# Minimum and maximum of the key gap moved from GpSimd to VectorE, with a new instruction order, in a fused recurrent block (RWKV attention gated by a feed-forward branch)

## The reference

```
xn = layernorm(x)                                  # over channels
shifted = xn moved one token later (zero first)
k, v, r = (xn*mix + shifted*(1-mix)) @ Wk, Wv, Wr  # three mixes
r = sigmoid(r)
# per channel, a scan over the 512 tokens, kept stable by a running maximum mx
td = -exp(time_decay)
out   = (e1*num + e2*v) / (e1*den + e2)            # e1 = exp(mx-max_out), e2 = exp(k+tf-max_out)
mx'   = max(mx + td, k)
num'  = exp(mx+td-mx')*num + exp(k-mx')*v
den'  = exp(mx+td-mx')*den + exp(k-mx')
s = (r * out) @ Wo
h = relu(xn @ w1[0] + b1[0]);  y = h @ w2[0] + b2[0]   # 128 -> 512 -> 128
g = silu(layernorm(xn + y) * gamma + beta)
result = x + s * g
```

## Time and profile before

| what | value |
|---|---|
| median of 3 runs | 134.46 us (133.47 to 134.66) |
| the profiled execution, its own time | 134.19 us |
| its span, first to last instruction | 132.4 us |
| busy: PE, DVE, ACT, POOL | 108.0, 104.2, 99.8, 93.3 us |
| mean granted TensorE clock | 0.955 |

### The profile page before, as it was taken

The page is one execution under the profiler, slowest core; times in us unless marked ns, Lnnn a source line. Parts: engine busy times, 40 slices in busy tenths (PEclk is TensorE's granted clock), DMA queues, the critical chain, the costliest instruction groups (busy, mean ns, idle before and its releaser), DMA issues. The chain is left out here.

```text
span 132.4 us, 1678 instructions
## 1 busy us (share of the span) xinstructions
PE 108.0 (82%) x340; PEld 57.8 (44%) x340; DVE 104.2 (79%) x208; ACT 99.8 (75%) x154; POOL 93.3 (70%) x124
## 2 busy tenths in 40 slices
...
DVE  1796988998449999387899997099956999887972
...
POOL 2069799999996799789969999999929428204000
...
GB/s 121 264 344 144 2 0 0 0 2 5 0 0 2 0 0 0 0 0 14 68 0 0 5 0 79 0 0 0 0 2 82 0 51 29 0 2 84 0 158 79
DMA packets 9450, 5.09 MB, mean 38 GB/s; under 512 B 480, under 2 KB 9184, under 8 KB 9440
## 3 DMA queue, kind: packets, MB, share of 16 engines
...
q10 hardware_dynamic: 560, 0.40, 1.1%
...
...
## 5 line engine op out<-in xcount | busy, mean ns | idle before, releaser
L620 PE MATMUL ps_z<-hid,w_c 128*128 128x512 f32 x64 | 30.8, 599 | 0.2 <-issue 0.2
L585 PE MATMUL ps_up<-xT_hi,w_hi 128*128 128x512 f32 x32 | 20.8, 651 | 7.2 <-POOL xT_hi L340 2.6
L445 ACT ACTIVATE hid<-ps_up,vec 128x512 f32<-128x512 f32 x32 | 21.1, 680 | 4.7 <-PE ps_up L587 4.6
L368 POOL TENSOR_SCALAR gap_max<-gap,td 128x512 f32<-128x512 f32 x8 | 16.6, 2072 | 1.7 <-DVE gap L745 1.2
L620 PEld LDWEIGHTS ps_z<-hid,w_c 128*128 128x128 f32 x64 | 11.4, 189 | 12.5 <-issue 9.5
L327 POOL TENSOR_SCALAR xn<-x_sb,neg_mean,rstd 128x128 f32<-128x128 f32 x28 | 15.0, 546 | 0.2 <-POOL rstd L313 0.2
L587 PE MATMUL ps_up<-xT_lo,w_hi 128*128 128x512 f32 x32 | 13.1, 409 | 0.0
L586 PE MATMUL ps_up<-xT_hi,w_lo 128*128 128x512 f32 x32 | 13.0, 406 | 0.0
L585 PEld LDWEIGHTS ps_up<-xT_hi,w_hi 128*128 128x128 f32 x32 | 6.5, 202 | 14.9 <-issue 9.5
L752 DVE TENSOR_TENSOR_SCAN den<-e_keep,e_new 128x512 f32<-128x512 f32 x8 | 10.5, 1312 | 2.4 <-ACT e_new L473 2.3
L376 POOL TENSOR_TENSOR dv<-v_sb 128x512 f32<-128x512 f32 x8 | 9.3, 1157 | 4.4 <-ACT v_sb L487 4.4
...
## 6 DMA issues: line engine op xcount, KB each, us to landing
...
```

The lines of the kernel that those rows point to most:

```text
L368: pool.tensor_scalar(gap_max[n][:, :], gap[n][:, :], td[:, :], HIGHEST, ALU.max, ALU.min).then_inc(done["gap_max"], 1)
L445: act.activation(hid[b % 2][:, f, :], ps_up[f % 2][:, :], ACT.Relu, bias=vec[:, B1_COLUMN + f:B1_COLUMN + f + 1]).then_inc(done[f"hid{f}"], 1)
L585: pe.matmul(dst, hi, xT_hi[n][:, :], start=True, stop=False)
L620: ins = pe.matmul(ps_z[b % 2][:, :], w2_c[:, f, :], hid[b % 2][:, f, :], start=False, stop=last, skip_group_check=True)
```

## The change

`gap_min` and `gap_max` leave POOL's list and go to DVE's, as one `tensor_scalar` each with one comparison instead of two. Their waits are the same. POOL's list has 70 steps in place of 86, DVE's 160 in place of 144; PE's and ACT's have as many steps as before (124 and 154, with the same 16 table loads). The order of the steps is new on all four engines. On POOL three waits are added that the new order needs. The diff, with the lists of PE and ACT cut:

```diff
 ACT = mybir.ActivationFunctionType
 LN_EPS = 1e-5
 MX_START = -1e38
-LOWEST, HIGHEST = -3.4028234e38, 3.4028234e38
 WARM_UP = 11
...
     "pe": """
-        T:0 b2m up0:0 up3:0 k:0 up2:0 up1:0 z3:0 z2:0 z0:0 T:1 z1:0 v:0 up1:1 var:0 up0:1 k:1 up3:1 r:0
...
+        b2m T:0 up0:0 up1:0 k:0 up2:0 up3:0 z1:0 z0:0 z3:0 T:1 z2:0 v:0 var:0 up2:1 up1:1 k:1 up0:1 r:0 T:2
...
     "act": """
-        ln_exp ve0 rs0 w1_hi neg_td xT:0 xT_hi:0 hid0:0 wo hid3:0 hid2:0 hid1:0 xT:1 e_keep:0 e_new:0 sq:0
...
+        ln_exp ve0 rs0 w1_hi neg_td xT:0 xT_hi:0 hid0:0 hid1:0 hid3:0 hid2:0 e_new:0 e_keep:0 wo xT:1 sq:0
...
     "dve": """
-        bnA:0 bnB:0 aggr1:0 norm1:0 bn:1 aggr1:1 one_minus cols xT_lo:0 w2_sum ink:0 bn:2 inr:0 aggr1:2
-        inv:0 mx:0 gap:0 bn:3 bn:4 aggr1:3 bn:5 xT_lo:1 den:0 ink:1 rel:0 inr:1 mx:1 zn:0 inv:1 aggr1:4
-        gap:1 dev:0 xT_lo:2 adev:0 ink:2 wkv:0 gated:0 inr:2 den:1 zn:1 rel:1 inv:2 mx:2 ink:3 gap:2 xT_lo:3
-        bn:6 inr:3 dev:1 aggr1:5 mx:3 gap:3 adev:1 wkv:1 inv:3 den:2 zn:2 bn:7 rel:2 aggr1:6 prod:0 den:3
-        xT_lo:4 res:0 ink:4 gated:1 dev:2 inv:4 adev:2 wkv:2 zn:3 inr:4 mx:4 rel:3 prod:1 gated:2 ink:5
-        aggr1:7 gap:4 dev:3 xT_lo:5 adev:3 wkv:3 inr:5 mx:5 gap:5 zn:4 res:1 inv:5 den:4 gated:3 ink:6 rel:4
-        xT_lo:6 prod:2 mx:6 dev:4 adev:4 gap:6 wkv:4 inv:6 den:5 inr:6 zn:5 den:6 res:2 rel:5 rel:6 xT_lo:7
-        ink:7 prod:3 dev:5 gated:4 mx:7 res:3 adev:5 gap:7 wkv:5 gated:5 inv:7 inr:7 prod:4 den:7 dev:6
-        adev:6 wkv:6 rel:7 res:4 zn:6 gated:6 prod:5 dev:7 prod:6 adev:7 wkv:7 res:5 gated:7 res:6 zn.a:7
-        zn.b:7 prod.a:7 prod.b:7 res.a:7 res.b:7
+        bnA:0 bnB:0 aggr1:0 one_minus norm1:0 bn:1 cols aggr1:1 w2_sum xT_lo:0 inv:0 ink:0 bn:2 inr:0 mx:0
+        bn:3 gap:0 aggr1:2 gap_min:0 gap_max:0 bn:4 aggr1:3 den:0 bn:5 xT_lo:1 inr:1 ink:1 rel:0 zn:0 inv:1
+        mx:1 aggr1:4 gap:1 dev:0 gap_max:1 ink:2 xT_lo:2 adev:0 gap_min:1 wkv:0 mx:2 gated:0 gap:2 den:1
+        gap_min:2 zn:1 gap_max:2 inr:2 inv:2 bn:6 prod:0 rel:1 den:2 xT_lo:3 ink:3 dev:1 aggr1:5 aggr1:6
+        adev:1 mx:3 wkv:1 rel:2 inr:3 zn:2 inv:3 gated:1 bn:7 gap:3 res:0 gap_min:3 gap_max:3 dev:2 xT_lo:4
+        adev:2 ink:4 wkv:2 inv:4 den:3 inr:4 zn:3 prod:1 rel:3 gated:2 mx:4 res:1 aggr1:7 gap:4 ink:5
+        xT_lo:5 gap_min:4 dev:3 gap_max:4 mx:5 prod:2 adev:3 gap:5 wkv:3 gap_min:5 gated:3 inr:5 zn:4 inv:5
+        gap_max:5 den:4 res:2 ink:6 rel:4 den:5 xT_lo:6 mx:6 dev:4 gap:6 adev:4 gap_min:6 wkv:4 inr:6 inv:6
+        gap_max:6 zn:5 prod:3 den:6 gated:4 res:3 rel:5 ink:7 rel:6 xT_lo:7 dev:5 prod:4 adev:5 mx:7 wkv:5
+        gap:7 res:4 gated:5 inr:7 gap_min:7 inv:7 prod:5 gap_max:7 dev:6 den:7 adev:6 wkv:6 rel:7 res:5
+        gated:6 zn:6 prod:6 dev:7 res:6 adev:7 wkv:7 zn.a:7 gated:7 zn.b:7 prod.a:7 prod.b:7 res.a:7 res.b:7
     """,
     "pool": """
-        w1_lo neg_mean1:1 Bk:0 Br:0 Bv:0 w2_c rstd1:1 norm1:1 gap_min:0 gap_max:0 xT_hi:1 neg_mean1:2 Bk:1
-        Br:1 rstd1:2 Bv:1 norm1:2 dv:0 keep:0 xT_hi:2 Br:2 Bk:2 gap_max:1 neg_mean1:3 gap_min:1 rstd1:3 Bv:2
-        norm1:3 dv:1 neg_mean1:4 Bk:3 Br:3 xT_hi:3 keep:1 rstd1:4 gap_max:2 gap_min:2 neg_mean1:5 Bv:3
-        gap_max:3 gap_min:3 norm1:4 dv:2 neg_mean1:6 Bk:4 xT_hi:4 rstd1:5 keep:2 Br:4 Bv:4 norm1:5 rstd1:6
-        Bk:5 keep:3 dv:3 xT_hi:5 gap_min:4 Br:5 Bv:5 neg_mean1:7 gap_max:4 norm1:6 gap_min:5 gap_max:5 dv:4
-        Br:6 Bk:6 xT_hi:6 rstd1:7 Bv:6 keep:4 norm1:7 gap_max:6 gap_min:6 dv:5 Bk:7 xT_hi:7 Br:7 keep:5 Bv:7
-        keep:6 gap_max:7 gap_min:7 dv:6 keep:7 dv:7
+        w1_lo Bv:0 Bk:0 Br:0 w2_c rstd1:1 neg_mean1:1 norm1:1 rstd1:2 neg_mean1:2 xT_hi:1 Br:1 Bk:1 Bv:1
+        norm1:2 dv:0 keep:0 neg_mean1:3 Bk:2 neg_mean1:4 xT_hi:2 rstd1:3 Br:2 Bv:2 rstd1:4 norm1:3 norm1:4
+        Br:3 xT_hi:3 Bk:3 dv:1 keep:1 Bv:3 rstd1:5 neg_mean1:5 norm1:5 keep:2 dv:2 xT_hi:4 neg_mean1:6 Bk:4
+        rstd1:6 Bv:4 Br:4 dv:3 xT_hi:5 Bk:5 keep:3 Br:5 Bv:5 norm1:6 neg_mean1:7 Bk:6 xT_hi:6 rstd1:7 dv:4
+        keep:4 Br:6 norm1:7 Bv:6 dv:5 Bk:7 Br:7 xT_hi:7 keep:5 Bv:7 keep:6 dv:6 keep:7 dv:7
     """,
 }
 
@@ -294,6 +292,7 @@
             pool.memset(minus_half[:, :], -0.5).then_inc(prep["consts"], 1)
             pool.memset(eps[:, :], LN_EPS).then_inc(prep["consts"], 1)
             pool.memset(averager[:, :], 1.0 / H).then_inc(prep["consts"], 1)
+            pool.wait_ge(prep["consts"], 3)
 
             def center_w2():
                 pool.wait_ge(got["w2"], 16)
@@ -308,6 +307,8 @@
                 n = b % 2
                 after(pool, "aggr1", b)
                 after_rows(pool, b - 2)
+                if b == 1:
+                    after(pool, "rstd1", 0)
                 pool.tensor_tensor(ve1[n][:, :], mv1[n][:, :, 1], eps[:, :], ALU.add).then_inc(done["ve1"], 1)
                 after(pool, "ve1", b)
                 pool.tensor_tensor(rstd1[n][:, :], ve1[n][:, :], minus_half[:, :], ALU.pow).then_inc(done["rstd1"], 1)
@@ -322,7 +323,7 @@
                 n = b % 2
                 after(pool, "neg_mean1", b - 1)
                 after(pool, "rstd1", b)
-                after(pool, "T", b - 2)
+                after(pool, "T", max(b - 2, 0))
                 for j in range(NT):
                     pool.tensor_scalar(xn[n][:, j, :], x_tile(b, j), neg_mean1[n][:, j:j + 1], rstd1[n][:, j:j + 1],
                                        ALU.add, ALU.mult).then_inc(done["norm1"], 1)
@@ -352,22 +353,6 @@
                                        ALU.mult, ALU.add).then_inc(done["B" + name], 1)
                 return step
 
-            def lower(b):
-                n = b % 2
-                once(pool, b, "cols", 4)
-                after(pool, "gap", b)
-                after(pool, "e_new", b - 2)
-                pool.tensor_scalar(gap_min[n][:, :], gap[n][:, :], td[:, :], LOWEST, ALU.min,
-                                   ALU.max).then_inc(done["gap_min"], 1)
-
-            def upper(b):
-                n = b % 2
-                once(pool, b, "cols", 4)
-                after(pool, "gap", b)
-                after(pool, "e_keep", b - 2)
-                pool.tensor_scalar(gap_max[n][:, :], gap[n][:, :], td[:, :], HIGHEST, ALU.max,
-                                   ALU.min).then_inc(done["gap_max"], 1)
-
             def value_steps(b):
                 n = b % 2
                 once(pool, b, "edges", EDGES)
@@ -384,7 +369,7 @@
                 pool.tensor_scalar(keep[n][:, 1:], th_g[n][:, :], -0.5, 0.5, ALU.mult, ALU.add).then_inc(done["keep"], 1)
 
             steps = {"w1_lo": w1_low, "w2_c": center_w2, "rstd1": inverse_std, "dv": value_steps, "xT_hi": high_part,
-                     "keep": kept, "norm1": normalise, "neg_mean1": minus_mean_rows, "gap_min": lower, "gap_max": upper}
+                     "keep": kept, "norm1": normalise, "neg_mean1": minus_mean_rows}
             steps.update({"B" + name: share_before(name) for name in "kvr"})
             run("pool", steps)
 
@@ -744,6 +729,18 @@
                     after(dve, step, b - 2)
                 dve.tensor_tensor(gap[n][:, :], ps_k[:, :], mx[n][:, 0:T], ALU.subtract).then_inc(done["gap"], 1)
 
+            def lower(b):
+                n = b % 2
+                after(dve, "gap", b)
+                after(dve, "e_new", b - 2)
+                dve.tensor_scalar(gap_min[n][:, :], gap[n][:, :], td[:, :], None, ALU.min).then_inc(done["gap_min"], 1)
+
+            def upper(b):
+                n = b % 2
+                after(dve, "gap", b)
+                after(dve, "e_keep", b - 2)
+                dve.tensor_scalar(gap_max[n][:, :], gap[n][:, :], td[:, :], None, ALU.max).then_inc(done["gap_max"], 1)
+
             def denominator(b):
                 n = b % 2
                 after(dve, "e_new", b)
@@ -817,7 +814,7 @@
 
             steps = {"bnA": first_stats(0), "bnB": first_stats(1), "bn": stats, "aggr1": aggregate, "norm1": normalise_first,
                      "one_minus": one_minus_mix, "cols": small_columns, "w2_sum": w2_row_sums,
-                     "xT_lo": low_part, "mx": running_max, "gap": exponents,
+                     "xT_lo": low_part, "mx": running_max, "gap": exponents, "gap_min": lower, "gap_max": upper,
                      "den": denominator, "rel": relative, "dev": deviation, "adev": weighted,
                      "wkv": mixed_values, "gated": gate, "zn": scale, "prod": multiply, "res": add_input}
             steps.update({"in" + name: mix(name) for name in "kvr"})
```

More of the change, by code:

```diff
@@ L32 @@
[L32 to L33 removed]
+        b2m T:0 up0:0 up1:0 k:0 up2:0 up3:0 z1:0 z0:0 z3:0 T:1 z2:0 v:0 var:0 up2:1 up1:1 k:1 up0:1 r:0 T:2
+        z1:1 up3:1 z2:1 z0:1 k:2 z3:1 up1:2 up0:2 var:1 up3:2 up2:2 s:0 T:3 v:1 z1:2 z0:2 z3:2 z2:2 up0:3
+        var:2 k:3 up1:3 back:0 r:1 v:2 up3:3 T:4 up2:3 z3:3 r:2 z0:3 z2:3 z1:3 up1:4 up0:4 var:3 v:3 s:1 k:4
@@ L34 @@
+        T:5 back:1 up2:4 z0:4 r:3 s:2 up3:4 z1:4 k:5 z2:4 z3:4 up1:5 up0:5 var:4 up3:5 up2:5 v:4 T:6 back:2
```

(14 more changed lines are left out.)

18 lines of the change are left out of this document (11 added, 7 removed).

## The result

The changed kernel takes **123.62 us** (median of 4 runs, 123.34 to 125.56) against 134.56 for the kernel before in the same comparison (4 runs, 133.47 to 135.41): ratio 0.9185, interval 0.9100 to 0.9269. The forecast was 131.0 with a range from 126.5 to 137.0. The profiled execution took 123.34 us with a span of 121.5.

What follows compares the result with a forecast made beforehand. The prediction took POOL's queue as the bound up to about 97 us, then DVE, PE and ACT together. It summed 134.19 - 13.1 removed + 9.8 added = 130.9 us, forecast as 131.0, range 126.5 to 137.0.

Steps and rivals of the forecast that it cites:

- the five stops: DVE waits before mixed_k, den and three zn, traced to gap_min and gap_max on POOL; all were to go, -11.7 us.
- the work added "in full": On DVE, all added instruction time and holding counted on top, 6.4 + 3.4 = 9.8 us, DVE being then the fullest engine.
- the other four: DVE stops from before_k, before_v and xT_hi coming late from POOL, 3.5 us, forecast to stay.
- The end, -0.5 us: At den of batch 7, DVE's 0.48 us wait for e_new was to vanish with both limits on DVE.
- one_minus, -0.9 us: At the start on DVE, placed before the first normalisation, it was to take 0.14 us instead of 1.01, gaining 0.9.
- Price of the instruction, 0.486 us, pitch 0.40: Each of 16 moved instructions on DVE takes 0.486 us and holds the queue 0.40, adding 6.4 us; upper end 10.6.
- Holding, 3.4 us: Each moved instruction on DVE waits on average 0.21 us for a running POOL instruction, 3.4 us for 16; bounds 0 and 11.0.
- The rival in which every instruction meets a whole POOL instruction: Each of the 16 on DVE waits 0.69 us for POOL, 11.0 in place of 3.4, giving 138.5 us; chance 0.14.
- The order: The new step order was credited only with one_minus placed early, 0.9 us, and the wait of den at the end, 0.5.
- The signs it named: New profile: DVE busy near 115 us, POOL near 70, no DVE slice under 7 from 15 to 125 us, one_minus 0.14.
- the one in which the order does better: The four remaining POOL stops (3.5 us) vanish and holding costs nothing (3.4): 124.1 us, halfway 127.5; chance 0.16.
- New waits in place of the old: All queues wait on DVE and part of zn's stops return: 134.2 us if 3.3 stay, 136.8 if 5.9; chance 0.22.

Runs made afterwards that it cites:

- the move alone: Kernel before, with gap_min and gap_max taken off POOL and put on DVE right behind each gap, all else in the old order: 128.35 us, ratio 0.9607.
- the slow pair on POOL: Kernel after in its new order, with gap_min and gap_max back on POOL in their old form: 132.97 us, ratio 0.9958 to the kernel before.
- the fast pair: New order with gap_min and gap_max on POOL, gap_max written min first and max second: 125.92 us, against 125.41 for that form in the old order.
- the kernel without the shares: Kernel after without POOL's 24 before_k, before_v and before_r instructions, the mixes reading xT instead, so the output differs: 120.16 us, ratio 0.8932.

## Why the prediction was right and where it was wrong

- **What bounds the kernel: right.** POOL's queue did. A cheaper comparison on POOL alone, with no step moved, took 8.5 us off, and the five stops that were named shrank from 11.7 us to 3.1.
- **Stops removed, 11.7 us, and the work added "in full": the step that failed.** "I leave the 3.5 us of the other four standing" was wrong for this change. The prediction was right that they weren't the five's: with the cheap form on POOL they stood unchanged at 3.5 us. But it added ten us of work to DVE and counted all of it on top, though some of that work stands ahead of the waits and fills them: DVE comes later to a before_k that is then ready, as the first of the four shows. In the move alone the four shrank to 1.0 us and the five to 0.7; DVE's idle time over the span fell by 15.3 us, against the 12.2 of the prediction, and by 15.9 with the new order.
- **The end, -0.5 us: not told apart.** The wait of den for e_new is gone (0.1 us over all eight). But DVE's idle time behind 110 us is 5.4 us in the 22.4 us left before and 4.6 in the 11.5 left after, which are not the same work, and no run isolates it.
- **one_minus, -0.9 us: right in its duration, less in its worth.** 0.14 us in the new place, 1.15 put back; the total moves by 0.2 us in each of two comparisons (1.2 and 0.2 by the ratios), neither of them outside the noise.
- **Price of the instruction, 0.486 us, pitch 0.40: right.** Undisturbed they take 0.45 to 0.49, and the next one starts 0.39 to 0.40 us after them; eight more of them cost 0.25 to 0.35 us each. The Trainium skill, "VectorE: DVE Perf Modes", section The perf-mode tier table, gives this operation two elements per cycle. The trace agrees: 0.475 us is near the 0.486 of that form and far from the 0.742 at the full price per element.
- **Holding, 3.4 us: half of it on the pair.** Their means, 631 and 529 ns, are 1.7 us over the plain value in all, where 3.4 was expected. In the move alone, where one_minus keeps its place, DVE's busy time rose by 9.1, near the 6.4 + 3.4 = 9.8 of the sum, but in part because rel became longer (704 to 984 ns, 2.2 us in all). So the total of this term came out right by luck, and its place was not. The Trainium skill's rule in "SBUF — State Buffer", section Who interferes with whom, that a Vector instruction in a 2-port mode and a GpSimd instruction shut each other out for the whole instruction, agrees with two meetings: one_minus put back ran from 7.90 to 9.05 us beside a w_lo that ended at 9.03, and the longest gap_min (1293 ns, from 100.61) met a dv on POOL from 100.59 to 101.62. The rival in which every instruction meets a whole POOL instruction fell: the mean wait is 0.11 us, and it needed 0.42.
- **The order: the second step that failed.** It was counted with one_minus and the end, 1.4 us together. It is worth 4.7 us (5.7 by the ratios) where DVE is the bound; with the slow pair on POOL 0.8, not clear of the noise, and nothing with the fast pair there. The prediction had itself counted 0.08 us of overlap between neighbours, and didn't ask whether gap's new neighbours could have it. 1.5 us of DVE's busy time came from overlap; that 2.6 came from shorter durations is shown, why these are shorter is not: fewer meetings with POOL's instructions fit, but with the rstd steps on ACT, where POOL does less, rel and den became longer.
- **The signs it named.** DVE's busy time is 109, not near 115. That 115 counted the sixteen at 0.49 us where the sum counts 0.40; by the sum's own terms it is 104.2 + 6.4 + 3.4 - 0.9 = 113.1, which the move alone has (113.3), and the order took off the rest. POOL is at 72.6 for 70. Three slices of DVE are under 7, all behind 109 us (6, 6 and the last, 2), in the tail that now begins earlier. e_keep and e_new no longer wait for POOL but for DVE, 1.5 and 1.9 us in all.
- **"Both are gone whatever the reason": a question left unasked.** The earlier trace rows had gap_max at 2.3 times gap_min for the same shape and operands. Following that would have shown that the load on POOL was mostly one form of instruction.

Idle and busy time of DVE make up the span, so the measured terms close by themselves: 134.19 - 15.3 + 9.1 = 128.0 for the move alone. Against the prediction's -12.2 and +8.9 the full change has -15.9 and +5.0, so of the 7.6 us that the sum lacks 3.7 are the stops and 3.9 DVE's busy time, which the order took off. Of the rivals, the one in which the order does better gave 124.1 and came nearest, for a reason half its own: the four stops did all but vanish (0.44 us before a mixed_v is left), the holding did not, and the order made up for it. New waits in place of the old didn't come: DVE is idle for 1.95 us between 20 and 110, where the prediction had set 8 as the mark. In the first 20 us the granted clock of TensorE was 0.91 in the kernel before and in the move alone and 1.00 after; DVE's idle time there (6.0, 6.0 and 5.8 us) shows no effect of it.

Open are the part of holding in the kernel without the shares (3.5 us faster; earlier inputs for mixed_k, mixed_v and mixed_r may account for some of it), and why the lighter POOL with the rstd steps on ACT left DVE's rel and den longer (dev was shorter, 1285 ns); ACT was busy for 1.6 us more in it, too.
